# ScalarE's order in a double step of an attention kernel: one copy ahead of the second exponential

## The reference

```
q = (einsum(x, Wq) + bq) / sqrt(64);  k = einsum(x, Wk) + bk;  v = einsum(x, Wv) + bv
attn = softmax(einsum('bqhd,bkhd->bhqk', q, k))
out = einsum('bhqk,bkhd->bqhd', attn, v);  y = einsum('bqhd,hdm->bqm', out, Wo) + bo
x = x + layernorm(y)
x = x + layernorm(gelu(layernorm(x) @ U1 @ V1 + b1) @ U2 @ V2 + b2)
```

## Time and profile before

| | us |
|---|---|
| Median of 3 runs | 2431.14 |
| Lowest and highest | 2429.1 and 2431.36 |
| Profiled execution, its own time | 2428.23 |
| Its span (first to last instruction) | 2426.4 |

### The profile page before, as it was taken

How to read it: one execution, slowest core, us unless ns; L and a number is a source line. 1 busy time by engine, 2 the same in 40 slices (tenths; PEclk the granted TensorE clock), 3 DMA queues, 4 the chain that set the end, 5 groups by cost and what they waited for, 6 DMA issues and landing times.

```text
span 2426.4 us, 44311 instructions
## 1 busy us (share of the span) xinstructions
PE 2378.9 (98%) x15788; PEld 1191.4 (49%) x15788; DVE 2022.9 (83%) x3174; ACT 2151.8 (89%) x2499; POOL 2032.2 (84%) x1145
## 2 busy tenths in 40 slices
PE   6999999999999999999999999999999999999997
PEld 3454545445455454544545454554545545444444
DVE  6888888888888888888888888888888888888865
ACT  5999899999999999999998989999999999998985
POOL 4888888888888888888888888888888888889984
PEclk8999999999999999999999999999999999999998
DMA  1000001000000000100000000100000000100101
GB/s 51 28 15 27 28 14 33 28 14 27 28 20 27 28 18 24 33 19 22 27 20 28 28 27 14 33 28 14 27 28 20 27 28 19 30 32 23 36 23 36
DMA packets 59902, 62.61 MB, mean 26 GB/s; under 512 B 25284, under 2 KB 43588, under 8 KB 59684
## 3 DMA queue, kind: packets, MB, share of 16 engines
q1 hardware_dynamic: 58676, 59.43, 8.0%
q10 hardware_dynamic: 1008, 0.33, 0.1%
HBM read 56.88 MB, written 2.61 MB: 25 GB/s over the span
## 4 chain that ended last, share of the span: by engine, by line
PE 92%; DVE 3%; POOL 2%; ACT 1%; issue 1%; DMA 0%; POOLq 0%; ACTq 0%; DVEq 0%
PE o_ps L435 35%; PE spare_ps L392 13%; PE score_ps L414 10%; PE score_ps L417 9%; PE score_ps L420 9%; PE spare_ps L378 3%; PE spare_ps L369 3%; PE spare_ps L485 3%; PE spare_ps L360 3%; POOL total L1116 2%; PE spare_ps L447 1%; DVE max_part L862 1%; PE spare_ps L399 1%; DVE ln_stats L828 1%; ACT probs L686 0%
## 5 line engine op out<-in xcount | busy, mean ns | idle before, releaser
L1116 POOL TENSOR_TENSOR total<-total,probs 128x832 f32<-128x832 f32 (+1 forms) x894 | 1758.7, 1967 | 297.4 <-ACT probs L686 222.0
L862 DVE TENSOR_REDUCE max_part<-spare_ps 128x1 f32<-128x512 f32 x2027 | 1303.2, 685 | 320.5 <-PE spare_ps L392 306.7
L686 ACT ACTIVATE probs<-score_ps 128x1024 f32<-128x1024 f32 x1024 | 993.1, 1023 | 218.4 <-PE score_ps L420 218.1
L676 ACT ACTIVATE score_ps<-m_all 128x1024 f32<-128x1024 f32 x1024 | 1010.2, 1028 | 5.2 <-DVE max_part L862 4.9
L435 PE MATMUL o_ps<-probs,v_sb 128*64 128x512 f32 x4096 | 986.9, 596 | 1.1 <-ACT o_sb L692 1.1
L435 PEld LDWEIGHTS o_ps<-probs,v_sb 128*64 128x64 f32 x4096 | 300.2, 137 | 386.3 <-issue 249.8
L392 PE MATMUL spare_ps<-k_hi,q_hi 64*128 64x512 f32 x2027 | 455.9, 445 | 13.7 <-DVE max_part L862 13.1
L414 PE MATMUL score_ps<-q_hi,k_hi 64*128 64x512 f32 x2048 | 426.0, 412 | 1.2 <-ACT score_ps L676 1.2
L420 PE MATMUL score_ps<-q_hi,k_lo 64*128 64x512 f32 x2048 | 405.2, 391 | 0.0
L417 PE MATMUL score_ps<-q_lo,k_hi 64*128 64x512 f32 x2048 | 404.4, 391 | 0.0
L392 PEld LDWEIGHTS spare_ps<-k_hi,q_hi 64*128 64x128 f32 x2027 | 193.1, 184 | 425.4 <-issue 245.2
(11 more groups left out here) (137 smaller groups left out, 978.8 us busy)
## 6 DMA issues: line engine op xcount, KB each, us to landing
m_all<-m_scratch SPq DMA_DIRECT2D x64, 512.0 KB, 3.7
denom<-denom_scratch SPq DMA_DIRECT2D x122, 128.0 KB, 2.9
y_acc<-in_L_attn_x SPq DMA_DIRECT2D x8, 256.0 KB, 5.9
xg<-in_L_attn_x SPq DMA_DIRECT2D x8, 256.0 KB, 3.0
block_out<-probs SPq DMA_DIRECT2D x8, 256.0 KB, 2.3
m_scratch<-max_rows SPq DMA_DIRECT2D x64, 4.0 KB
denom_col<-denom SPq DMA_DIRECT2D x61, 4.0 KB
denom_scratch<-denom_col SPq DMA_DIRECT2D x61, 4.0 KB, 1.4
```

The source lines that it names most:

```text
L676: nc.scalar.activation(score_ps[st % 2][:], m_all[:, G % 2], ACT.Copy).then_inc(s["seed_done"], 1)
L686: nc.scalar.activation(probs[:, st % RING], score_ps[st % 2][:], ACT.Exp, scale=SCALE).then_inc(s["exp_done"], 1)
L862: nc.vector.reduce_max(max_part[:, G % 2, h, qt, kc:kc + 1], bank[max_bank(n, h)], AX.X).then_inc(s["max_done"], 1)
L1116: nc.gpsimd.tensor_tensor(others(total[:, G % 2], G), so_far, others(probs[:, st % RING], G), ALU.add).then_inc(s["sum_done"], 1)
```

## The change

In each double step ScalarE issues the copy for step 2n+2 between the two exponentials; before, it came after both of them and after the evacuation. The copy for step 2n+3 stays where it was. No semaphore, count or buffer changes, and no other engine's queue.

```
                 act_exp(act, 2 * n)
+                if n + 1 < DOUBLES:
+                    act_seed(act, 2 * n + 2)
                 act_exp(act, 2 * n + 1)
                 if keys_at(u, c, d):
                     act_k(act, *keys_at(u, c, d))
...
                 if d == M_AT and G + 1 < CHUNKS:
                     act_m(act, G + 1)
                 if n + 1 < DOUBLES:
-                    act_seed(act, 2 * n + 2)
                     act_seed(act, 2 * n + 3)
```

## The result

The changed kernel takes 2469.3 us at the median of 4 runs, beside 2430.1 for the kernel before (4 runs): a ratio of 1.016, 95% interval 1.0143 to 1.0178. That is 39 us, where I had forecast 27. The profiled execution took 2466.0 us with a span of 2464.2, 37.8 more than the span before.

What follows compares the result with a forecast made beforehand. TensorE's stream was taken as the bound, ScalarE counting only where it makes that stream wait. Second-copy stalls of 23 us plus 4 us for the maxima's transfer made 27 us: 2458 us, 1.1% slower, range 2442 to 2483.

Steps and rivals of the forecast that it cites:

- ScalarE's side: ScalarE's double step: first copy 1.06 behind its exponential, second exponential at 2.01, second copy at 3.07 in place of 2.77.
- E: Start of the first exponential of a double step on ScalarE, from which the prediction counts that step's times in us.
- The stalls: TensorE waiting for the later second copy, at d = 0, 4, 5 and 7: 1.42 us a unit, 23 us for 16 units.
- the transfer: Maxima's transfer at a chunk's last double step (d = 7): every sixth or seventh of 63 boundaries late by 0.7; 4 us.
- the reading of the room: Slack before TensorE's second score product, from second copy's end, less 0.05; stall is lateness less room less the previous stall.
- the forecast's own bounds: 2445 us, if the stalls are half and the transfer costs nothing, to 2468 us.
- The own wait is dearer: Rival: ScalarE's wait for its predecessor ends 0.08 to 0.12 past the end, not 0.04; 2471 to 2483 us; chance 0.13.
- The transfer as limit: Rival: maxima's transfer holds the first copy 0.7 late at every chunk boundary; 37 us, 2495 us; chance 0.10.
- The own wait is free: Rival: waiting for one's own predecessor costs nothing, only the transfer's few microseconds stay; 2431 to 2435 us; chance 0.07.
- Faster: Rival: a quarter of TensorE's 72.7 us of load waits for copies gained by the earlier first copy; 2413 us; chance 0.03.

Runs made afterwards that it cites:

- the run with the added wait: Kernel before, order unchanged, with one wait added: the first copy waits for the second exponential just ahead of it; 2439.4 us, ratio 1.0038.

## Why the prediction was right in its direction and too small in size

**ScalarE's side** came out as written: copy 1.05 behind its exponential (1.06), second copy at E + 3.08 (3.07), no loss at d = 1, 2, 3 and 6 to speak of. Nothing came from GpSimd or from VectorE, though VectorE's wait for the keys' high part rose from 23.4 to 84.9 us: TensorE's other stretches stayed as they were to 0.02 us. The first copy, 0.76 earlier, bought nothing.

**The stalls** came out as well: 1.42 for the second copy and 4 us / 16 = 0.25 for the transfer were forecast per unit, together 1.67; from product to product the trace has 1.59. They came out part by part too. In ten ordinary units (the second to the sixth, the tenth to the fourteenth) the stalls are 1.23: 0.44 behind d = 0 (forecast 0.53), 0.24 behind d = 4 (0.23), 0.24 behind d = 5 (0.37), 0.27 behind d = 7 (0.29) and 0.04 behind d = 2 (nothing). The transfer I come to below.

**The step that failed** is the reading of the room, "from the end of the second copy to the start of that product, less the 0.05 that the signal needs". What waits for the copy is the weight load, which in the free case runs 0.23 ahead of the product. Two things follow. A room of 0.03 (643.84) was none: the product there is drawn 0.47 long in place of 0.39, which I had in front of me and didn't read, and the kernel before already paid for it. Its load starts only 0.03 ahead:

```profile
643.81 0.19 PEld L414 LDWEIGHTS score_ps<-q_hi,k_hi 64*128 64x128 f32 x2 [0.24 <-ACT score_ps L676]
```

And each load that is newly late has 0.10 to 0.12 behind it that isn't seen as a stall. That term, absent from my sum, measured 0.71 us a unit, 11 us in all (9.4 if only the distance to the very next product is added up).

27 + 11 = 38 agrees with the span's 37.8 better than it has a right to: 16 ordinary units would have grown by 31 us and the transfer adds 4; the rest is 3 us more in the first unit, which nothing in my sum stands for, and small differences in the last two. The time, too, lies inside my range only because the range took in the dearer wait; the forecast's own bounds, 2445 to 2468, end 1 us below it.

**The rivals.** *The own wait is dearer*: no, 0.03 past the end. It would have given 2471 to 2483, near the time measured, for a wrong reason; the copy's distance in the timeline tells the two apart. *The transfer as limit*: no, and making it later still changed nothing. Of the 12.3 us of waits for it 4.7 stand before the first copy of all, where the kernel before waits 4.9 for VectorE; the other 7.6 are at 11 of the 63 boundaries, where I had estimated every sixth or seventh and 6 us. Nine of the 11, 6.6 us, lie in the seventh to the ninth unit. At seven of these nine the denominators' transfers come later, and the maxima's behind them are issued 1.2 to 1.8 us after the evacuation, in place of 0.15 to 0.4 as at most others. These three units grew by 3.25 us on average, the ordinary ones by 1.95, and with the old order at d = 7 they grew by 1.91: so the transfer costs 4 us, the term of my sum. *The own wait is free*: refuted by the run with the added wait. *Faster*: no; the load of a first group started with its product (within 0.01) 13 times in the kernel before and 11 times now, so there was next to nothing to win there.

What stays open: why the first unit lost 5 us rather than 2, and why the denominators' transfers come later in the middle units.

## What to carry to other kernels

Room in front of a product is measured at its weight load, which here starts 0.23 us ahead of it when nothing holds it: a load that was held until 0.10 ahead still cost nothing behind it, one that was held until the product's own start cost 0.10. A product drawn longer than its fellows is one whose load was late. Putting an instruction directly behind the one it waits for costs its overlap, 0.15 us of ScalarE here, and the time grew by it though ScalarE wasn't the bottleneck; something independent between them (the second exponential, an evacuation) made the wait free. And where two buffers are filled in turn and consumed together, it is the last one's time that counts: an earlier first one buys nothing, and work that isn't urgent goes behind the last.

## What I had not expected of the hardware

A small copy to DRAM issued right behind two transfers of 128 KB came back after 2.08 us, and issued 0.77 us later after 1.46, so that the delay was nearly free; with nothing large ahead of it, it came back after 1.2. A pair of 512-column products whose weight loads could not run ahead was drawn 0.50 rather than 0.39 us long, and held up what follows by 0.10 to 0.12, on a TensorE whose busy share stayed at 98% while 38 us were lost.
